# Ternary weights on GpSimd and lighter VectorE passes in a two-layer attention and feed-forward kernel on one core

## The reference, cut to what matters

```
x = x + mlstm_cell(layernorm(x), ctx, ctx)           # 4 heads of 64; gates from x and ctx
x = x + layernorm(x) @ (ternary(w0) * mean|w0|).T    # 256 x 256
x = x + softmax((layernorm(x) Wq)(ctx Wk).T / 16) (ctx Wv)
x = x + bitlinear(silu(bitlinear(h, w_gate)) * bitlinear(h, w_up), w_down),  h = layernorm(x)

ternary(w)      = clip(round(w / max(mean|w|, 1e-5)), -1, 1)
bitlinear(a, w): rows of a are rounded to steps of max(max|a|, 1e-5) / 127,
                 w is ternary(w) * mean|w|;  w_gate, w_up: 1024 x 256, w_down: 256 x 1024
```

## Time and profile before

| | |
|---|---|
| time, median of 3 runs | 703.07 us (701.47 to 704.61) |
| profiled execution, its own time | 703.04 us |
| its span, first to last instruction | 701.3 us |
| mean granted TensorE clock | 0.983 of full |
| busy: PE, DVE, ACT, POOL | 655.5, 609.0, 518.3, 391.8 us |
| chain that ended last: PE, DVE, ACT, issue | 53%, 30%, 10%, 4% |
| first part up to the first feed-forward matmul | 0 to 488.3 us |
| feed-forward blocks and their drain | 488.3 to 701.3 us |

### The profile page before, as it was taken

How to read it: one execution, slowest core, us unless ns; L and a number is a source line. 1 busy time by engine, 2 the same in 40 slices (tenths; PEclk the granted TensorE clock), 3 DMA queues, 4 the chain that set the end, 5 groups by cost and what they waited for, 6 DMA issues and landing times.

```text
span 701.3 us, 15286 instructions
## 1 busy us (share of the span) xinstructions
PE 655.5 (93%) x4958; PEld 493.9 (70%) x4958; DVE 609.0 (87%) x1661; ACT 518.3 (74%) x1203; POOL 391.8 (56%) x556
## 2 busy tenths in 40 slices
PE   5889999999999999999999999998899999999996
PEld 4668778686867868788787787876465666666664
DVE  4787989888898887989889889897999999999994
ACT  4556677686767668787777787865588889888885
POOL 3366564362735445574574555652366667666665
PEclk9999999999999999999999999999999999999999
DMA  8310202122020312202212121014123424425221
GB/s 290 102 44 18 91 1 92 48 74 90 17 92 16 91 46 76 91 16 91 77 47 91 45 78 61 17 56 155 50 85 94 143 79 122 120 81 158 84 78 61
DMA packets 72659, 55.54 MB, mean 79 GB/s; under 512 B 20093, under 2 KB 72318, under 8 KB 72582
## 3 DMA queue, kind: packets, MB, share of 16 engines
q1 hardware_dynamic: 64134, 50.37, 23.7%
q10 hardware_dynamic: 8448, 4.20, 2.0%
HBM read 29.39 MB, written 20.97 MB: 72 GB/s over the span
## 4 chain that ended last, share of the span: by engine, by line
PE 53%; DVE 30%; ACT 10%; issue 4%; POOL 1%; DMA 1%; DVEq 0%; POOLq 0%; ACTq 0%
PE bank L690 10%; PE bank L637 8%; PE bank L658 8%; PE bank L607 5%; PE bank L707 5%; DVE C L1513 4%; DVE hmax L1516 4%; DVE st L1200 3%; PE bank L679 3%; PE bank L699 3%; PE bank L575 3%; ACT ew L852 2%; PE bank L566 2%; PE bank L512 2%; DVE x L1359 2%
## 5 line engine op out<-in xcount | busy, mean ns | idle before, releaser
L690 PE MATMUL bank<-WGU,fqT 128*128 128x512 bf16 x512 | 125.0, 382 | 4.0 <-DVE C L1513 3.4
L1074 POOL TENSOR_SCALAR_AFFINE_SELECT D<-D 128x512 f32<-128x512 f32 x64 | 38.4, 636 | 124.9 <-ACT D L843 124.9
L1059 POOL TENSOR_TENSOR rs<-ve,minus_half 128x4 f32<-128x4 f32 x64 | 65.3, 1026 | 47.5 <-DVE ve L1206 47.0
L1513 DVE SCALAR_TENSOR_TENSOR C<-bank,fback,D 128x1024 f32<-128x1024 f32 x64 | 81.9, 1280 | 7.4 <-ACT D L989 5.5
L690 PEld LDWEIGHTS bank<-WGU,fqT 128*128 128x128 bf16 x512 | 48.0, 98 | 57.0 <-DVE C L1513 17.3
L989 ACT ACTIVATE D<-bank,fback 128x1024 f32<-128x1024 f32 x64 | 71.1, 1111 | 15.6 <-PE bank L690 15.3
L1516 DVE TENSOR_REDUCE hmax<-C 128x1 f32<-128x1024 f32 x64 | 78.1, 1220 | 2.2
L993 ACT ACTIVATE fhT<-bank 128x1024 f16<-128x1024 f16 x64 | 65.5, 1023 | 19.5 <-PE bank L699 18.2
L1152 POOL TENSOR_SCALAR wtmp<-C,hscale 128x1024 f32<-128x1024 f32 x64 | 71.6, 1119 | 0.4 <-issue 0.4
L707 PE MATMUL bank<-WD,fhT 128*128 128x256 f16 x512 | 66.3, 273 | 0.3 <-ACT fhT L993 0.3
L1200 DVE BATCH_NORM_STATS2 st<-x 128x6 f32<-128x256 f32 x180 | 63.1, 413 | 2.6
(11 more groups left out here) (198 smaller groups left out, 1514.2 us busy)
## 6 DMA issues: line engine op xcount, KB each, us to landing
out_dram<-x SPq DMA_DIRECT2D x31, 512.0 KB, 3.3
xg<-in_x_dram SPq DMA_DIRECT2D x16, 512.0 KB, 3.9
cg<-in_ctx_dram SPq DMA_DIRECT2D x16, 512.0 KB, 4.5
rows_q<-fq ACTq DMA_DIRECT2D x16, 256.0 KB, 2.2
xg<-out_dram SPq DMA_DIRECT2D x8, 512.0 KB, 5.1
cg<-out_dram SPq DMA_DIRECT2D x8, 512.0 KB, 5.0
raw<-in_L_ffn_w_gate_dram SPq DMA_DIRECT2D x1, 1024.0 KB, 7.9
nrm<-in_L_ffn_w_up_dram SPq DMA_DIRECT2D x1, 1024.0 KB, 10.3
```

Source lines behind the costliest of these rows:

```text
L690: mm = pe.matmul(ps[k + half], fqT[:, s, c, :], WGU[:, c, which, half * 512:(half + 1) * 512], start=(c == 0), stop=(c == EC - 1))
L1513: dve.scalar_tensor_tensor(out=fh[:, s % 2, :], in0=up, scalar=fback[:, p, s % FB, 1:2], in1=fsil[:, s % 2, :], op0=ALU.mult, op1=ALU.mult ...
```

## The change

- Ternary weights: DVE keeps w0 only. POOL gets a `ternary(n)` with the three passes of one matrix behind each other, after the `vaug` passes of a turn: w_gate in the WS turn, w_up at z = 0, w_down at z = 1. PE and ACT turn and copy w_gate at z = 0 as before, w_up at z = 1 and w_down at z = 2.
- Variance plus epsilon: from DVE's `statistics` to POOL's `power`, four times in a turn.
- Heads: the division by 64 is folded into head_scale (times 8), one DVE pass less. Gates: |f| and max(-f, 0) are made by ACT (Abs, Relu) in place of three DVE passes. Row steps: five small passes become three.
- Feed-forward: the guard 1e-5 is a constant column behind the product's 1024 columns, which the maximum reads too; DVE takes the reciprocal of the maximum, and POOL multiplies by 127 (a new small pass) and makes the scale back. The product's two buffers are now two of the vg tiles.
- The last groups: group 14's statistics are made before block 0, its power and shifts on POOL ahead of the blocks; DVE's row work comes at every other block; x3 of group 15 comes in halves after blocks 0 and 1, and PE waits for the four banks one by one. In the drain POOL scales two head blocks before `power(3, 13)` and two after.

```diff
-WEIGHTS_AT = {0: "WG", 3: "WU", 6: "WD"}
-TERNARY_AT = {0: (1, 2), 1: (2, 0), 2: (2, 1), 3: (2, 2), 4: (3, 0), 5: (3, 1), 6: (3, 2)}
+WEIGHTS_AT = {0: "WG", 1: "WU", 2: "WD"}
...
+        fh = [flat(vg[k])[:, 0:INNER + 1] for k in (1, 2)]
...
 # scalar, in turn, behind the T2 copies
-                    act.wait_ge(gstep, 4 * n + 3)
+                    act.wait_ge(gstep, n + 1)
+                    act.activation(gabs[:, :, :], gates[:, :, NH:], ACT.Abs).then_inc(g_exp, 1)
+                    act.activation(gneg[:, :, :], gates[:, :, NH:], ACT.Relu, scale=-1.0)
+                    act.wait_ge(g_exp, 2 * n + 1)
                     act.activation(gexp[:, :, :], gabs[:, :, :], ACT.Exp, scale=-1.0).then_inc(g_exp, 1)
...
 # gpsimd, power()
+                pool.wait_ge(aggr[i], GB * group + GB)
+                pool.tensor_scalar(ve[i][:, :], mv[i][:, :, 1], LN_EPS, 64.0 if i == 0 else 1.0,
+                                   ALU.add, ALU.mult).then_inc(veps[i], 1)
...
+            def ternary(n):
+
+                w, done = w_raw[n], 2 * n - 2
+                if n == 1:
+                    pool.wait_ge(means_ready, 1)
+                pool.tensor_scalar(w, w, mean_inv[:, n:n + 1], ROUND, ALU.mult, ALU.add).then_inc(wstep, 1)
+                pool.wait_ge(wstep, done + 1)
+                pool.tensor_scalar(w, w, ROUND, 1.0, ALU.subtract, ALU.min).then_inc(wstep, 1)
+                pool.wait_ge(wstep, done + 2)
+                pool.tensor_scalar(w_tern[n], w, -1.0, None, ALU.max).then_inc(tern, 1)
...
 # gpsimd, end of turn()
+                if "WS" in bank.stages:
+                    ternary(1)
+                if z in (0, 1):
+                    ternary(z + 2)
...
 # gpsimd, last_rows(i) and each block
+                if i == 35:
+                    power(3, NG - 1)
+                if i == 36:
+                    shifts(3, NG - 1)
+            def product_scales(i):
+                s = i % FB
+                pool.wait_ge(f_hinv, i + 1)
+                pool.tensor_scalar(hscale[:, s:s + 1], hinv[:, s:s + 1], 127.0, None, ALU.mult).then_inc(f_hs, 1)
+                if i >= FB:
                     pool.wait_ge(o_clear, i - 1)
+                pool.tensor_scalar(hback[:, s:s + 1], hmax[:, s:s + 1], mean_abs[:, 3:4], 1.0 / 127.0,
                                    ALU.mult, ALU.mult).then_inc(f_hback, 1)
...
 # vector
             x3_rows(fore, NG - 2, x2, x3)
+            statistics(3, x3, NG - 2)
...
                 if i == 0:
                     inverse(aft, NG - 1)
-                    x3_rows(aft, NG - 1, x2_last, x3_last)
+                    x3_rows(aft, NG - 1, x2_last, x3_last, (0, 1))
+                if i == 1:
+                    x3_rows(aft, NG - 1, x2_last, x3_last, (2, 3))
+                for group, at in ((NG - 3, 2), (NG - 2, 20), (NG - 1, 38)):
+                    if i in range(at, at + 2 * GB, 2):
+                        row_max(group, ((i - at) // 2,))
+                    if i == at + 2 * GB:
                         row_scales(group)
+                    if i == at + 2 * GB + 2:
                         row_back(group)
+                if i in (14, 16, 18, 32):
+                    row_statistics(x3_last, (14, 16, 18, 32).index(i))
+                if i == 34:
+                    row_variance(NG - 1)
...
                 dve.wait_ge(f_hm, i + 1)
-                dve.tensor_scalar(hstep7[:, s % FB:s % FB + 1], hmax[:, s % FB:s % FB + 1], Q_EPS, 1.0 / 127.0,
-                                  ALU.max, ALU.mult).then_inc(f_hstep, 1)
-                dve.wait_ge(f_hstep, i + 1)
-                dve.reciprocal(hscale[:, s % FB:s % FB + 1], hstep7[:, s % FB:s % FB + 1]).then_inc(f_hs, 1)
+                dve.reciprocal(hinv[:, s:s + 1], hmax[:, s:s + 1]).then_inc(f_hinv, 1)
```

More of the change, by code:

```diff
@@ L369, in build @@
         fore, aft = last_places()
[L371 to L376, removed]
         @block.sync
@@ L437, in _, with group_out, ffn_block @@
             sp.dma_start(grp(out, NG - 1), x3_last[:, :, :]).then_inc(x_out, 16)
[L439 to L464, removed]
+            def group_out(g):
+                sp.wait_ge(f_done, FB * g + FB)
+                sp.dma_start(grp(out, g), fo[g % 2][:, :, :]).then_inc(f_out[g % 2], 16)
+                if g + 4 < NG:
+                    sp.dma_start(fx[g % 4], grp(out, g + 4)).then_inc(f_in[g % 4], 16)
+            def ffn_block(i):
+                if i + FB < B:
+                    hold("sp", sp, u_full, i + 1)
+                    rows_turned(i + FB, i % FB)
+                if i % FB == FB - 1 and i >= FB:
+                    group_out(i // FB - 1)
+            for i in range(B):
+                if i == FB * (NG - 6):
+                    sp.wait_ge(x_out, 16 * NG)
+                for g in range(NG - 3, NG):
+                    if i == FB * (g - 1):
+                        sp.wait_ge(q_out, 16 * (g + 1) + 16)
+                ffn_block(i)
+            group_out(NG - 1)
             for p in range(2):
@@ L720, in _ @@
             turn(aft.part("O"), None, None, NG - 1, None, None, 1, (NG + 1) % 3)
[L722 to L739, removed]
+            for i in range(B):
+                if i > 0:
+                    gate_up(i, i % FB, i // FB)
+                if i in (2, 3):
+                    last_rows_out(i - 2)
+                if i > 1:
+                    product_rows(i - 2, i % 2)
+                if i in (3, 4):
+                    last_rows_out(i - 1)
+                if i > 2:
+                    down(i - 3)
+            product_rows(B - 2, 0)
+            down(B - 3)
+            product_rows(B - 1, 1)
+            down(B - 2)
+            down(B - 1)
         @block.scalar
@@ L1124, in _ @@
             power(1, NG - 2)
+            scale_heads(fore, 0)
+            scale_heads(fore, 1)
             power(3, NG - 3)
             shifts(3, NG - 3)
-            for b in range(GB):
-                scale_heads(fore, b)
+            scale_heads(fore, 2)
+            scale_heads(fore, 3)
             head_power(NG - 1)
@@ L1178, in _ @@
+            for i in range(B):
+                product_scales(i)
+                ffn_round(i)
+                if i > 2:
+                    ffn_out(i - 3)
+                last_rows(i)
+            for i in range(B - 3, B):
+                ffn_out(i)
         @block.vector
@@ L1390, in turn @@
                     means(bank)
-                    for step in range(3):
-                        ternary(0, step)
+                    ternary_w0()
                 if y is not None:
@@ L1528, in ffn_turn @@
-            def ffn_turn(g, p, first, last):
-                for s in range(FB):
-                    i = FB * g + s
-                    ffn_mul(i, s, g, p % 2)
-                    row_scale(i, s)
-                    if s == 1 and not last:
-                        scales(g + 1, 1 - p % 2)
-                    last_rows(i)
-            feed_forward(dve, ffn_turn)
+                dve.reciprocal(hinv[:, s:s + 1], hmax[:, s:s + 1]).then_inc(f_hinv, 1)
+            for k in range(2):
+                dve.memset(fh[k][:, INNER:INNER + 1], Q_EPS).then_inc(f_guard, 1)
@@ L1541 @@
+            for i in range(B):
+                ffn_mul(i)
+                if i % FB == 1 and i < B - FB:
+                    scales(i // FB + 1, (i // FB + 1) % 2)
+                last_rows(i)
 _INS = ['x', 'ctx_1024', 'L0_xattn_igate_w', 'L0_xattn_igate_b', 'L0_xattn_fgate_w', 'L0_xattn_fgate_b',
```

246 lines of the change are left out of this document (99 added, 147 removed).

## The result

The changed kernel took **721.9 us** (four runs, 721.3 to 725.0) beside 702.5 for the kernel before on the same chip: a ratio of 1.028, 95% interval 1.024 to 1.032. The forecast of 691.0 was wrong in sign. The profiled execution, on which what follows is read, has a span of 723.3 us and its own time is 725.04, 22.0 over the profiled one of before; it is the slowest of the four, 3.1 above their median.

What follows compares the result with a forecast made beforehand. Steady turns were taken as two loops of nearly one length, PE's and one over ScalarE and DVE. Sum: -2.8 - 10.1 + 4.0 + 1.5 - 0.3 - 1.0 - 3.8 + 0.5 = -12.0, from 703.0 to 691.0 us; range 679 to 700.

Steps and rivals of the forecast that it cites:

- the price of one ternary pass: GpSimd's tensor_scalar over 2048 elements: 1.97 by straight line, 2.24 in proportion, 2.05 us taken with the gap.
- Rival (c): In-place fp32 ternary passes run at GpSimd's two-input pace; at 4.5 us each, 713 us; sign: over 3.4; chance 0.06.
- The hold: WS turn, z = 0 and 1: GpSimd's three ternary passes hold VectorE's short passes behind vaug, +5.0 us a turn.
- the 7 foretold: Sign: VectorE's six passes from scan to mT take near 7 us in the WS turn, z = 0 and 1.
- rival (b): Steady turns gain nothing, and the hold is longer or catches VectorE's two 1024-element passes before the scan: 698 us; chance 0.18.
- Steady turns: Turns z = 7 to 13 fall from 27.84 to 27.4 us as C starts earlier: -2.8 us together.
- in front of PE's TX: Steady turns: two added GpSimd passes delay ScalarE's qn by about 0.7 us, which PE's room covers: booked at nothing.
- its 28.4: Turn z = 2, which carries w_down's stage: 27.4 and 1.0, so 28.4 us.
- The clock: PE's waits for spl in three turns may lower the granted clock: +1.5 us for the three.
- Blocks: Feed-forward blocks: one VectorE pass less, row work every other block, -3.8 us; sign: blocks 3 to 63 take 183 to 184.
- the start: Start of the blocks: x3 in halves lets block 1's product start earlier, -1.0 us.
- The stall at block 37: Group 15's power and shifts at blocks 35 and 36 may make ScalarE wait about 1 us once: +0.5 us.

Runs made afterwards that it cites:

- experiment 5: The kernel of experiment 3, with GpSimd's ternary passes made to wait until VectorE's mT of the same turn is out: 691.2 us.
- experiment 4: The changed kernel with the later ternary passes on GpSimd written in other operations, one set for each weight, same values: 730.6 us (one run).
- experiment 3: The changed kernel with GpSimd's second ternary pass as (mult, add) and third as (min, max), same values: 703.3 us.
- experiment 1: The changed kernel with the ternary passes back on VectorE, one at a time at the turns of before: 690.6 us.
- Experiment 6: The kernel of experiment 1, with power(0) and its shifts put ahead of power(1) on GpSimd: 683.7 us.
- experiment 7: The kernel of Experiment 6, with VectorE's ternary pass moved beside its wait for the logarithm and group 15's power and shifts a block earlier: 677.9 us.

## Why the prediction was wrong

**The step that failed** is the price of one ternary pass, 2.05 us, and the words it rests on: "One is a tensor_scalar over 2048 elements. The same form over 1024 takes 1.119". The row was a (mult, add), and the prediction took the instruction's name and shape for its form, for three passes of which two had other operations. The straight line from it was exact for its own case: 1.97 forecast, 1.98 measured in experiment 5. For (subtract, min) the pass took 7.1 to 7.9, for max 5.37. Rival (c) had the consequence, at a chance of 0.06: 0.9 us for each 0.1 us in a pass; its sign, a pass over 3.4, came. Its reason, that in-place fp32 passes run at the pace of two inputs, does not hold: in place over fp32 (min, max) took 1.89 in experiment 4 and (mult, add) 1.90 in experiment 3. The mean pass of the changed kernel is (2.89 + 7.94 + 5.37) / 3 = 5.40, 3.35 over the 2.05 assumed; 691 + 30 = 721, beside 721.9. That it meets so closely is luck. In the profiled execution the WS turn and z = 0 and 1 run over their forecast by 6.8 and 17.9, 24.7 together and not 30, and the steady turns from z = 7 and the blocks are off by 7 more between them.

**The hold** was right in kind, and in size at the pass length assumed, though not by the passes named. Experiment 3 is the changed kernel with passes of 1.9 to 3.0. Against experiment 1 its first F0 comes 5.1 us later, and z = 0 and 1 last 4.0 and 4.9 longer (+5.0 forecast for each). From scan to mT it is 6.7 us in the WS turn, near the 7 foretold, in place of 1.9. But in z = 0 and 1 it is 5.1, and there VectorE's add of 1024 elements before the scan is caught too, 2.88 in place of 1.23, which the prediction had only in rival (b). In the changed kernel the span from scan to mT is 13.4 us in the WS turn and 13.1 in z = 0. Experiment 5 takes the overlap away and the hold with it. Here the Trainium skill's rule in "SBUF — State Buffer", "Who interferes with whom", holds: a pass moved to GpSimd isn't out of VectorE's way when VectorE works from two SBUF inputs or in a two-port mode. In that section the Trainium skill puts "for the whole instruction" with the two-port modes, and says of two SBUF inputs only that they contend with GpSimd's reads; the prediction took both for one. The traces show a difference of that kind: beside the long passes, the two-input ones were let go early. In z = 0 of the changed kernel the scan ended at 92.16 with GpSimd's pass running to 94.47, and r at 98.33 with the pass running to 99.92, while both casts ended within 0.1 of GpSimd's passes. In experiment 3, with passes of 1.9, the held casts, r and scan all ended within 0.3 of GpSimd's. That the two-input passes escaped early is part of why the loss is 24.7 and not 30; how much was not measured.

**Steady turns**: 27.4 forecast, 28.12 measured. The named step is "in front of PE's TX, which has about that much room, so I put nothing". Measured from the end of the cut the delay is the 0.7 foreseen (3.34 in place of 2.55 us), most of it the two new passes in front with their gaps. But behind F0 qn comes 1.45 later, for F0 now starts as the cut ends (347.50) and no longer 0.67 behind it, and the room was less than that. Experiment 6 takes power(1) from ahead of qn's shifts: 27.51. That the two variance passes by themselves make the difference was not tested alone. z = 2 at 28.38 met its 28.4, but as 28.12 and 0.26 for w_down's stage, not as 27.4 and 1.0.

**The clock** was put at +1.5 for three turns. PE's own busy time grew by 3.1 in z = 0, and z = 1 has 2.6 more than z = 2 with the same products (30.58, 27.97), with a granted clock of 0.84 and 0.88 where it had been 1.00. From 103 to 107 us, behind PE's wait of 10.09, it is 0.50, the 1.2 GHz level. Part is hidden beside VectorE's delay, so no single price can be read here. Between runs of one kernel the time goes with it: experiment 3 at 0.992 and at 0.98 lie 5 to 6 us apart. A hold isn't needed for it: in experiment 5 the clock is 0.50 from 56.57 to 60.00, behind the wait of 4.28 for C.

**Blocks**: the start gave -1.1 (-1.0 forecast). The stall at block 37 was foreseen at 0.5, with the right waiter, and cost 1.5. Counted from block 5, -3.1 of the remaining -3.8 came. The sign given for it did not: blocks 3 to 63 were to take 183 to 184 us, and from silu to silu they take 186.8, as before. The first three blocks gain 2.7, more than forecast, and blocks 3 to 5 give 1.6 of it back. Over all blocks it is -2.7 in place of -4.3.

**What stays open**: why (min, max) is fast and (max, min) slow is not known from these runs. What Abs and Relu on ScalarE are worth was not measured alone. With the passes that VectorE shed, its wait before nlf went from 0.40 to 1.10 us, and experiment 7 fills it. Nor was it tried whether fast forms, GpSimd's later start and the orders of experiments 6 and 7 together would beat 677.9.

## What to carry to other kernels

When work is moved to another engine, find a row with the same *operations*, not only the same instruction and shape; where there is none, the bound is the slowest row of any form, and one instruction timed by itself settles it before the order of the kernel is built around it. A pass on GpSimd is cheap for VectorE only beside work that it doesn't hold, so place it behind the short passes that others wait for, and see that the engine's next pass that others wait for doesn't come late by it. An engine's small passes count by their place in its queue: with two of 0.19 us put ahead of the shifts that ScalarE waits for, a turn that was to gain 0.4 us lost 0.3, and changing the order of two steps gave 6.8 us back.

## What the runs showed of the hardware

- GpSimd's tensor_scalar over 128 x 2048 fp32: (mult, add) 1.90 to 1.98 us in experiment 5, where none began during VectorE's 1024-element passes, (min, max) 1.89; mult, min or max alone 5.37; (max, min), (max, mult), (add, min) and (subtract, min) 7.08 to 7.11. Add alone (6.23) and (subtract, mult) (7.95) were seen only where VectorE's add of 1024 elements brings some 0.85 more. Two fast operations in one pass cost a third of one alone.
- The hold works both ways. The first ternary pass lasted 2.89 to 3.13 when it began during one of VectorE's 1024-element passes with two SBUF inputs, longer by 0.9 to 1.15 us, about what was left of that pass, and 1.98 when it came behind them. The add that began during GpSimd's pass lasted 2.88 in place of 1.23.
- Behind PE's waits of 10.09 us (changed kernel, z = 0) and 4.28 us (experiment 5) the granted clock was 0.50. Over whole runs of experiment 3 a clock of 0.98 in place of 0.992 went with some 6 us more, as much as experiment 5 gained directly (5.6).
